# A fused attention and mixture-of-experts layer: keys and queries copied from SBUF into the stacks directly, and the experts' first gathers placed inside the last shared batch

## The chip, the cores and the metric

The kernel runs on 1 core of one Trainium2 chip. The metric is the device time of one execution in microseconds (us). PE is TensorE, DVE is VectorE, ACT is ScalarE, POOL is GpSimd and SP is SyncE, which here only issues DMAs.

## The reference

Input x has 8 sequences of 512 tokens with 512 features, all in float32.

```
h = layernorm(x)
c_kv, c_q = h @ W_DKV + b, h @ W_DQ + b                 # 128 wide each
k, q, v = c_kv @ W_UK + b, c_q @ W_UQ + b, c_kv @ W_UV + b   # 16 heads of 32
k_r, q_r = (h @ W_KR + b) * pe, (h @ W_QR + b) * pe     # 32 wide, shared by all heads
scores = concat(q, q_r) . concat(k, k_r) / sqrt(32)
x = x + layernorm(softmax(scores) @ v @ W_O + b)
h = layernorm(x)
shared = relu2(h @ shared_up) @ shared_down             # 512 -> 1024 -> 512
s = sigmoid(h @ router.T); pick 2 of 16 experts per token (2 of 4 groups first, by s + e_bias)
routed = sum over the 2 picked experts e of weight_e * relu2(h @ w_up[e]) @ w_down[e]   # 512 -> 256 -> 512
x = x + layernorm(routed + shared)
```

relu2 is the square of relu.

## The kernel before

**Stages.** Attention runs over 8 batches of 4 head groups (4 heads each), 32 groups u in all. Then the shared FFN runs over the first 4 batches ("shared batches"), the experts run over 79 tiles of 128 token rows sorted by expert, and the shared FFN of the last 4 batches runs together with the combination of the routed rows and the output. Products are made exact to nearly float32 by splitting operands into a high part (float32r) and a low part: three matmuls (`thrice`) for one.

**The order.** `K.order` is one list of steps, made by `attention_order`, `first_order`, `experts_order` and `combine_order`. Every engine's program walks the same list and issues its own instructions of each step, so the list sets the order on each engine and queue; semaphores do the rest. In attention `STEP` gives each side task the score step (0 to 31 within a group) beside which it stands; in the shared FFN `FIRST_STEP` gives it the number of the step (12 to a batch: 8 up-products, 4 down-products) after which it stands. Both tables are numbers written by hand or by a search.

**Keys and queries.** `half(u, "k")` and `half(u, "q")` make a group's K and Q on PE; ACT writes the high part and DVE the low part into `K.kq`, a single buffer [128, 4, 512]. Partition p = 32 j + d holds feature d of head j. The scores need stacks: `K.Kc` and `K.Qc`, three of each, with 128 partitions that are three 32-row pieces (high, high, low for K; high, low, high for Q) and 32 rows of the rotated part, for each of the 4 heads. `send(u)` on SP makes one: it copies `K.kq` to `kq_scratch` in DRAM (L1743), copies the rotated rows into the stacks (L1748, L1749) and, once the first copy has landed, reads the six pieces back in the new arrangement (L1753). Before the copies at L1748 it waits for the rotated part (`Z.rope`), which for the first group of a batch DVE makes (L888) while the third group of the batch before runs. ACT may write K of the next group into `K.kq` once the copy to DRAM has landed. `top(u)` (L614) multiplies queries and keys for the row maxima, which DVE reduces (L908); `scores(u)` (L628, L633) makes the scores, ACT the exponentials (L1404), POOL their sums (L1594).

**Choosing and inverting.** Beside the four shared batches DVE picks the experts ("choose early"), and computes every token's slot ("choose late"). Then eight steps "invert rows" (`spread`: L1218 to L1221 on DVE, eight small products of L757 on PE each) turn slots into the list of tokens for each expert tile, and "index" writes it (L1225). In the shared FFN L707 is the up-product (12 matmuls each), L729 the down-product (24 matmuls each); DVE makes the low part of each squared activation at L977.

**Experts.** `fetch(i)` on POOL gathers the 128 rows of a tile from DRAM (L1663), `move(i)` on SP copies them in four pieces within SBUF (L1828), DVE transposes (L1234), PE multiplies (L775, L798), the result goes to DRAM. Four buffers of each. The first fetches wait until the list is written and the up-products of the fourth shared batch are done, since their buffer lies in those activations' tile; the first transposition waits for the last down-product (`Z.dn`). Weights of the experts are loaded in groups: 0 and 1 (seven experts) beside the shared FFN, 2 and 3 (two experts each) at "weights 2" and "weights 3" on SP, the rest from ACT during the first ten tiles. The wait of a fetch and the head of `experts_order`:

```
        if i < 4:
            w.wait_ge(Z.idx, 1)
            w.wait_ge(Z.up, 8 * FIRST)
    out = [("fetch", i) for i in range(4)] + [("move", 0), ("move", 1)]
```

POOL also issues `store(b, i)`, which writes each shared result to DRAM (L1655) from one of two buffers; ACT waits for such a store before it reuses the buffer.

## Time and profile before

| | us |
|---|---|
| three runs, median (lowest to highest) | 1627.57 (1626.06 to 1628.75) |
| the profiled execution, its own time | 1631.91 |
| span of its profile | 1630.1 |
| PE busy in it | 1521.8 |
| DVE, ACT, POOL busy | 972.7, 786.2, 800.4 |
| mean granted clock of PE | 0.967 of full |

A busy share is a mean over stages with different limits. Attention lasts until about 909 us, the first four shared batches until 1115, the experts until about 1425, the rest is the second half of the shared FFN with the combination. In timelines the columns are start, duration, engine, line, operation, output and inputs, count; in brackets the idle time of the engine just before and what ended it. PEld is PE's weight load, SPq SP's DMA issues.

### The profile page before, as it was taken

How to read it: one execution, taken by the hardware profiler on the slowest of the kernel's cores; microseconds unless marked ns; L12 is line 12 of the kernel's file. 1: busy time of each engine (PE TensorE's matmuls, PEld its weight loads, DVE VectorE, ACT ScalarE, POOL GpSimd, SP SyncE). 2: the span in 40 equal slices, each digit the busy share in tenths (PEclk: the TensorE clock that was granted, in tenths of full speed). 3: DMA queues.
4: the chain of work that ended last, by engine and by line, in shares of the span. 5: the costliest groups of instructions: out<-in, count | busy, mean ns of one | idle time of the engine just before them, and what ended most of it. 6: DMA issues, size and time to landing. Idle time of an engine off the chain costs nothing.

```text
span 1630.1 us, 21821 instructions
## 1 busy us (share of the span) xinstructions
PE 1521.8 (93%) x7006; PEld 1034.3 (63%) x7006; DVE 972.7 (60%) x1871; ACT 786.2 (48%) x1417; POOL 800.4 (49%) x820
## 2 busy tenths in 40 slices
PE   4799999999999999999998999996899999969997
PEld 3465666656656566566564677875566666657886
DVE  3567676676756676757567336831333333339998
ACT  2355566456565665656647353430222222255554
POOL 1076696777776967768579430002222222133331
PEclk9799999999999999999999999998999999989999
DMA  4657358376483783745833334307977777596773
GB/s 118 192 146 203 101 163 253 104 223 175 129 223 107 196 253 113 214 142 150 279 106 105 129 129 144 109 20 246 289 215 214 213 224 211 160 338 221 225 233 130
DMA packets 169415, 291.32 MB, mean 179 GB/s; under 512 B 20596, under 2 KB 72692, under 8 KB 163156
## 3 DMA queue, kind: packets, MB, share of 16 engines
q1 hardware_dynamic: 150280, 242.21, 48.8%
q0 software_dynamic: 12912, 41.82, 8.7%
q10 hardware_dynamic: 6112, 5.90, 1.3%
q8 instruction: 58, 0.95, 0.2%
q14 instruction: 53, 0.43, 0.1%
HBM read 154.07 MB, written 92.01 MB: 151 GB/s over the span
## 4 chain that ended last, share of the span: by engine, by line
PE 75%; DMA 9%; DVE 4%; issue 4%; SPq 3%; POOL 3%; ACT 2%; DVEq 0%; POOLq 0%; ACTq 0%
PE bank L113 14%; PE bank L729 9%; PE bank L707 8%; PE bank L775 8%; PE bank L798 8%; PE bank L614 7%; PE bank L628 6%; PE bank L633 6%; PE bank L644 5%; DMA a<-kq_scratch 4%; PE bank L653 2%; SPq L1753 2%; POOL a L1594 2%; DMA kq_scratch<-a 1%; DMA f<-f 1%
## 5 line engine op out<-in xcount | busy, mean ns | idle before, releaser
L1594 POOL TENSOR_TENSOR a<-a 128x512 f32<-128x512 f32 x384 | 498.5, 1330 | 108.0 <-PE bank L653 68.6
L1404 ACT ACTIVATE a<-bank 128x512 f32<-128x512 f32 x512 | 298.4, 598 | 235.4 <-PE bank L633 183.8
L908 DVE TENSOR_REDUCE a<-bank 128x1 f32<-128x512 f32 x512 | 324.3, 680 | 79.5 <-PE bank L614 77.2
L113 PE MATMUL bank<-a 128*128 128x512 f32 (+1 forms) x864 | 245.0, 410 | 6.1 <-DVE a L854 4.0
L628 PE MATMUL bank<-a 128*128 128x512 f32 x512 | 222.0, 434 | 4.4 <-ACT a L1404 4.3
L614 PE MATMUL bank<-a 128*128 128x512 f32 x512 | 182.8, 429 | 29.6 <-DMA a<-kq_scratch 28.0
L633 PE MATMUL bank<-a 68*128 68x512 f32 x512 | 206.4, 403 | 0.7 <-ACT a L1394 0.6
L113 PEld LDWEIGHTS bank<-a 128*128 128x128 f32 (+1 forms) x864 | 166.0, 194 | 55.3 <-issue 10.3
L707 PE MATMUL bank<-c 128*128 128x512 f32 x768 | 181.4, 396 | 13.3 <-ACT c L1453 7.3
L729 PE MATMUL bank<-c 128*128 128x512 f32 x768 | 181.4, 396 | 4.5 <-DVE c L977 2.4
L1663 POOL DMA_INDIRECT f<-h_scratch,f x79 | 76.1, 963 | 208.5 <-DMA f<-f 206.6
L707 PEld LDWEIGHTS bank<-c 128*128 128x128 f32 x768 | 146.1, 191 | 48.0 <-issue 9.8
L729 PEld LDWEIGHTS bank<-c 128*128 128x128 f32 x768 | 145.7, 191 | 37.2 <-DVE c L977 3.3
L775 PE MATMUL bank<-f 128*128 x632 | 152.6, 385 | 17.9 <-DVE f L1234 16.6
L775 PEld LDWEIGHTS bank<-f 128*128 128x128 f32 x632 | 120.9, 193 | 70.2 <-issue 57.4
L628 PEld LDWEIGHTS bank<-a 128*128 128x128 f32 x512 | 98.4, 192 | 88.5 <-ACT a L1404 45.7
L614 PEld LDWEIGHTS bank<-a 128*128 128x128 f32 x512 | 98.4, 198 | 88.2 <-DMA a<-kq_scratch 32.2
L798 PE MATMUL bank<-f 128*128 x316 | 148.5, 593 | 0.0
L644 PE MATMUL bank<-a 128*32 128x512 f32 x1024 | 133.4, 607 | 0.0
L1242 DVE TENSOR_TENSOR f<-f 128x256 f32<-128x256 f32 x79 | 33.4, 423 | 138.1 <-ACT f L1518 138.0
L633 PEld LDWEIGHTS bank<-a 68*128 68x128 f32 x512 | 98.4, 192 | 18.8 <-ACT a L1394 4.8
L1528 ACT COPY f<-bank 128x512 f32<-128x512 f32 x79 | 46.3, 586 | 122.1 <-PE bank L798 122.1
(185 smaller groups left out, 1750.1 us busy)
## 6 DMA issues: line engine op xcount, KB each, us to landing
a<-kq_scratch SPq DMA_DIRECT2D x192, 256.0 KB, 5.7
kq_scratch<-a SPq DMA_DIRECT2D x32, 1024.0 KB, 4.1
a<-a SPq DMA_DIRECT2D x80, 256.0 KB, 5.4
f<-f SPq DMA_DIRECT2D x316, 64.0 KB
yp_scratch<-f SPq DMA_DIRECT2D x79, 256.0 KB, 3.2
a<-in_L_attn_x SPq DMA_DIRECT2D x15, 1024.0 KB, 8.4
x_scratch<-a SPq DMA_DIRECT2D x8, 1024.0 KB, 6.8
h_scratch<-a SPq DMA_DIRECT2D x8, 1024.0 KB, 12.4
```

Of the source, the lines that this page charges most:

```text
L113: t = e.matmul(out, a[n], b[n], start=n == 0 and m == 0, stop=n == len(ah) - 1 and m == 2)
L614: e.matmul(MX[n % 3][:], K.Qc[z][:, j, i * P:(i + 1) * P], K.Kc[z][:, j, :], start=True, stop=True).then_inc(Z.top, 1)
L628: e.matmul(SC[n % 2][:], K.Kc[z][:, j, i * P:(i + 1) * P], K.Qc[z][:, j, :], start=True, stop=False)
L633: e.matmul(SC[n % 2][:], K.KR[0:68, b % 2, j, i * P:(i + 1) * P], K.QR[0:68, u % 2, :], start=False, stop=True).then_inc(Z.score, 1)
L644: t = e.matmul(CT[HD * j:HD * j + HD, :], K.v[:, u % VS, i, HD * j:HD * j + HD], K.pt[:, n % NP, :], start=i == 0, stop=i == 3)
L707: t = e.matmul(bank[:], (K.sul if a else K.suh)[:, k, cut], (K.hTl if c else K.hTh)[:, k, :], start=m == 0, stop=m == 11)
L729: t = e.matmul(bank[:], (K.aTl if a else K.aTh)[:, k, cut], (K.sdl if c else K.sdh)[:, k, :], start=m == 0, stop=m == 23)
L775: t = e.matmul(K.UP[z][:, 0:FI], K.hTt[:, z, k * P:(k + 1) * P], K.flat[:, bass.ds(reg[i] + k * FI, FI)], start=k == 0, stop=k == 3)
L798: t = e.matmul(K.DN[z][:], K.eaT[:, z, k * P:(k + 1) * P], K.flat[:, bass.ds(reg[i] + 4 * FI + k * D, D)], start=k == 0, stop=k == 1)
L908: e.tensor_reduce(K.mx[:, i, j:j + 1], K.MX[n % 3][:], AX.X, ALU.max).then_inc(Z.max, 1)
L1404: e.activation(K.pt[:, n % NP, :], K.SC[n % 2][:], ACT.Exp, scale=SCALE).then_inc(Z.exp, 1)
L1594: e.tensor_tensor(K.acc[:, j, :], a, K.pt[:, n % NP, :], ALU.add).then_inc(Z.acc, 1)
```

## The change

The round trip through `kq_scratch` is gone. The columns of W_UK, W_UQ and their biases are permuted on the host so that partition p = 4 d + j holds feature d of head j; then a copy of 128 rows onto 32 partitions of four rows each is in the stack's order. `send(u)` first waits for the stack's last use, copies K's three pieces when K is drained, Q's three when Q is drained, and the two rotated copies last. ACT writes K of the next group only when all eight copies of the last stack have landed. The four first fetches, the weights of groups 2 and 3 and three moves are steps of `first_order` now (steps 40 to 45, in the fourth shared batch), with the weights issued by POOL instead of SP. All eight inversions stand at steps 33 to 35. Moves run three tiles ahead instead of two. Both tables of numbers are new.

```
@@ FIRST_STEP, STEP (numbers of most tasks differ by 0 to 5)
-        "weights": (44, 52, 56), "invert": (33, 33, 35, 35, 44, 44, 45, 45, 49)}
+        "weights": (37,), "invert": (33, 33, 34, 34, 34, 35, 35, 35, 37), "fetch": (40, 40, 40, 40, 41, 41, 41, 45, 45)}
@@ def first_order():
-                        ("early", [("choose early", 2)] * 26), ("late", [("choose late", 2)] * 34), ("weights", [("weights", n) for n in range(1, 4)]),
-                        ("invert", [("invert rows", n) for n in range(NCHUNK)] + [("index",)])):
+                        ("early", [("choose early", 2)] * 26), ("late", [("choose late", 2)] * 34), ("weights", [("weights", 1)]),
+                        ("invert", [("invert rows", n) for n in range(NCHUNK)] + [("index",)]),
+                        ("fetch", [("fetch", i) for i in range(4)] + [("weights", 2), ("weights", 3)] + [("move", i) for i in range(3)])):
@@ def experts_order():
-    out = [("fetch", i) for i in range(4)] + [("move", 0), ("move", 1)]
+    out = []
...
-            if i + 2 < NTILE:
-                out.append(("move", i + 2))
+            if i + 3 < NTILE:
+                out.append(("move", i + 3))
@@ scalar_program, half
-            w.wait_ge(Z.kq[(u - 1) % RS], 16 * ((u - 1) // RS + 1))
+            w.wait_ge(Z.stack[(u - 1) % RS], 8 * 16 * ((u - 1) // RS + 1))
@@ gpsimd_program
+    def weights(n):
+        if n < 2:
+            return
+        w.wait_ge(Z.inv, NCHUNK)
+        if n == 3:
+            w.wait_ge(Z.up, 8 * FIRST)
+        for e_ in range(E):
+            if GROUP[e_] == n:
+                for half in range(2):
+                    load_expert(e, K, ins, e_, half).then_inc(Z.ew[n], 16)
@@ sync_program, send
-        drained("half", u, "k")
-        drained("half", u, "q")
         if u >= RS:
             w.wait_ge(Z.stack[z], 8 * 16 * (u // RS))
-        e.dma_start(K.kq_d[z], raw(K.kq[:])).then_inc(Z.kq[z], 16)
+            w.wait_ge(Z.score, 16 * (u - RS + 1))
+        drained("half", u, "k")
+        for k, n in ((0, 0), (1, 0), (2, 1)):
+            e.dma_start(raw(K.Kc[z][HD * k:HD * k + HD, :, :]), raw(K.kq[:, n, :])).then_inc(Z.stack[z], 16)
+        drained("half", u, "q")
+        for k, n in ((0, 2), (1, 3), (2, 2)):
+            e.dma_start(raw(K.Qc[z][HD * k:HD * k + HD, :, :]), raw(K.kq[:, n, :])).then_inc(Z.stack[z], 16)
         rep = lambda r: raw(K.krx[r:r + HD, y, :].unsqueeze(1).broadcast_to([HD, 4, S]))
         w.wait_ge(Z.rope, 3 * (b + 1))
-        if u >= RS:
-            w.wait_ge(Z.score, 16 * (u - RS + 1))
         e.dma_start(raw(K.Kc[z][96:128, :, :]), rep(0)).then_inc(Z.stack[z], 16)
         e.dma_start(raw(K.Qc[z][96:128, :, :]), rep(32)).then_inc(Z.stack[z], 16)
-        piece = lambda n: K.kq_d[z, :, n, :].rearrange("(j p) s -> p j s", j=4)
-        w.wait_ge(Z.kq[z], 16 * (u // RS + 1))
-        for t, k, n in ((K.Kc, 0, 0), (K.Kc, 1, 0), (K.Kc, 2, 1), (K.Qc, 0, 2), (K.Qc, 1, 3), (K.Qc, 2, 2)):
-            e.dma_start(raw(t[z][HD * k:HD * k + HD, :, :]), piece(n)).then_inc(Z.stack[z], 16)
@@ sync_program, weights: groups 2 and 3 are gone
@@ kernel
+    for n in ("L0_attn_W_UK", "L0_attn_W_UQ", "L0_attn_b_UK", "L0_attn_b_UQ"):
+        given[n] = np.ascontiguousarray(given[n].reshape(-1, NG, 4, HD).swapaxes(2, 3).reshape(given[n].shape))
```

On SP, where the stack of a batch's first group is made (`a` are attention's tiles), before:

```order
L1743 DMA kq_scratch<-a 128x2048
L1748 DMA a<-a 32x4x512
L1749 DMA a<-a 32x4x512
L1753 DMA a<-kq_scratch 32x4x512 x6
L1727 DMA a<-a 32x4x512
L1728 DMA a<-a 32x4x512
L1717 DMA a<-in_L_attn_x 128x4x512
```

and now:

```order
L1753 DMA a<-a 32x4x512 x3
L1756 DMA a<-a 32x4x512 x3
L1759 DMA a<-a 32x4x512
L1760 DMA a<-a 32x4x512
L1736 DMA a<-a 32x4x512
L1737 DMA a<-a 32x4x512
L1726 DMA a<-in_L_attn_x 128x4x512
```

The six pieces stand ahead of the two rotated copies (L1759, L1760) and of the wait before them. On PE from the down-products of the third shared batch to the first expert tile, before:

```order
L729 MATMUL bank<-c 128x512 x48
L757 MATMUL bank<-h 128x79 x16
L729 MATMUL bank<-c 128x512 x48
L757 MATMUL bank<-h 128x79 x16
L707 MATMUL bank<-c 128x512 x96
L729 MATMUL bank<-c 128x512 x24
L757 MATMUL bank<-h 128x79 x16
L729 MATMUL bank<-c 128x512 x24
L757 MATMUL bank<-h 128x79 x16
L729 MATMUL bank<-c 128x512 x48
L773 TENSOR_LOAD f
```

and now:

```order
L730 MATMUL bank<-c 128x512 x48
L758 MATMUL bank<-h 128x79 x16
L730 MATMUL bank<-c 128x512 x24
L758 MATMUL bank<-h 128x79 x24
L730 MATMUL bank<-c 128x512 x24
L758 MATMUL bank<-h 128x79 x24
L708 MATMUL bank<-c 128x512 x96
L730 MATMUL bank<-c 128x512 x96
L774 TENSOR_LOAD f
```

All eight inversions (64 small products) stand in the third batch, none in the fourth. On POOL at the same place, before:

```order
L1655 DMA sh_scratch<-c 128x512 x12
L1663 DMA f<-h_scratch,f 128x512 x79
```

and now:

```order
L1653 DMA sh_scratch<-c 128x512 x8
L1661 DMA f<-h_scratch,f 128x512 x4
L547 DMA f<-in_L_ffn_w_up 128x4x256
L547 DMA f<-in_L_ffn_w_down 128x2x512
...
L1653 DMA sh_scratch<-c 128x512 x4
L1661 DMA f<-h_scratch,f 128x512 x75
```

Four gathers and eight weight loads (four pairs, of which one is shown) stand ahead of the fourth batch's four stores.

## Rows read from the trace of the kernel before

**Rows 1.** The page, busy time of each engine.
```profile
PE 1521.8 (93%) x7006; PEld 1034.3 (63%) x7006; DVE 972.7 (60%) x1871; ACT 786.2 (48%) x1417; POOL 800.4 (49%) x820
```
**Rows 2.** Who waited for whom on PE: us in all, times, longest.
```profile
PE bank L614 <- DMA a<-kq_scratch: 28.0, 10, 4.9
PE bank L729 <- DVE c L977: 2.4, 2, 1.4
```
**Rows 3.** Timeline, the prologue.
```profile
46.51 1.27 ACT L1387 ACTIVATE a<-bank,a 128x512 fp32r<-128x512 f32 x2 [1.00 <-DMA kq_scratch<-a]
...
53.83 2.29 DVE L854 TENSOR_TENSOR a<-s,a 128x2048 fp32r<-128x2048 f32 x1 [1.30 <-ACT a L1340]
...
56.75 9.54 PE L614 MATMUL bank<-a 128*128 128x512 f32 x16 [4.95 <-DMA a<-kq_scratch]
...
57.58 9.66 DVE L908 TENSOR_REDUCE a<-bank 128x1 f32<-128x512 f32 x16 [1.47 <-PE bank L614]
...
72.67 1.22 PE L614 MATMUL bank<-a 128*128 128x512 f32 x2 [2.81 <-DMA a<-kq_scratch]
```
**Rows 4.** Timeline, the end of attention, PE and POOL.
```profile
861.43 1.65 PE L614 MATMUL bank<-a 128*128 128x512 f32 x3 [2.99 <-DMA a<-kq_scratch]
...
870.07 1.28 POOL L1601 TENSOR_TENSOR s<-s,a 128x512 f32<-128x512 f32 x1 [1.18 <-DVE a L920]
```
**Rows 5.** Timeline of PE, from the shared FFN to the experts.
```profile
1103.47 11.15 PE L729 MATMUL bank<-c 128*128 128x512 f32 x48
...
1127.85 3.78 PE L775 MATMUL bank<-f 128*128 x8 [13.23 <-DVE f L1234]
...
1173.41 1.99 PE L775 MATMUL bank<-f 128*128 x8
```
**Rows 6.** Timeline of SP's queue, the stack of a batch's first group.
```profile
229.46 0.34 SPq L1743 DMA_DIRECT2D kq_scratch<-a  x1
236.55 0.60 SPq L1748 DMA_DIRECT2D a<-a  x1
...
237.84 3.86 SPq L1753 DMA_DIRECT2D a<-kq_scratch  x6
```
**Rows 7.** Timeline of PE, where that stack is asked for.
```profile
249.31 1.55 PE L614 MATMUL bank<-a 128*128 128x512 f32 x3 [2.53 <-DMA a<-kq_scratch]
```
**Rows 8.** DMA issues (KB each, median us to landing); landing times of all that touch kq_scratch.
```profile
a<-a SPq DMA_DIRECT2D x80, 256.0 KB, 5.4
...
DMA to landing us min/median/max: 3.5/5.5/13.0
```
**Rows 9.** The chain of waits around that stall: start, us, what.
```profile
231.73 2.78 PE bank L113 x12
...
250.85 2.37 PE bank L113 x6
```
**Rows 10.** Windows: PE, PEld, DVE, ACT, POOL busy, clock, DMA share, GB/s.
```profile
246.00:256.00 10.00, 7.47 (x34) 5.07 (x31) 4.58 (x8) 4.45 (x8) 3.26 (x3) 0.83 1.06 301
```
**Rows 11.** Timeline, inversions in the third and fourth shared batch.
```profile
1053.76 11.14 PE L729 MATMUL bank<-c 128*128 128x512 f32 x48
...
1055.43 1.22 DVE L1218 TENSOR_TENSOR h<-f 128x1024 f16<-128x1024 f32 x1
...
1070.20 0.69 DVE L977 TENSOR_TENSOR c<-c 128x512 fp32r<-128x512 f32 x1 [11.97 <-ACT c L1486]
...
1095.41 0.48 PE L757 MATMUL bank<-h 128*128 128x79 f16 x8 [2.23 <-DVE h L1221]
1095.72 7.30 PE L729 MATMUL bank<-c 128*128 128x512 f32 x24
```
**Rows 12.** The chain of waits, two expert tiles at full pace.
```profile
1184.66 1.73 PE bank L775 x8
...
1188.33 1.73 PE bank L775 x8
```
**Rows 13.** Timeline of POOL, the last store of the shared FFN.
```profile
1115.54 0.54 POOL L1655 DMA_DIRECT2D sh_scratch<-c  x1 [4.90 <-ACT c L1495]
```

More of the change, by code:

```diff
@@ L146 @@
 FIRST_STEP = {
-        "rest": (2, 2, 2, 3, 2, 2, 2, 3, 3, 5, 4, 5, 5, 7, 5, 6, 9, 9, 4, 9, 9, 9, 11, 9, 9, 9, 10, 10, 10, 10, 10, 10, 11, 13),
-        "prepare": (29,),
-        "early": (13, 13, 14, 14, 14, 14, 14, 15, 16, 17, 17, 18, 20, 20, 20, 20, 20, 20, 20, 21, 27, 28, 29, 31, 33, 35),
-        "late": (22, 22, 22, 22, 22, 22, 22, 22, 22, 22, 22, 23, 23, 23, 24, 24, 25, 25, 25, 25, 25, 25, 27, 27, 27, 27, 28, 28, 28, 29, 30, 30, 30, 36),
-        "weights": (44, 52, 56), "invert": (33, 33, 35, 35, 44, 44, 45, 45, 49)}
-STEP = {"split up": (4, 13, 17, 22, 25, 29, 36, 41), "split h": (38, 39, 42, 43), "last values0": 9, "total0": 8, "invert0": 5,
[11 rows of a table removed]
+        "rest": (1, 2, 2, 2, 2, 2, 3, 3, 3, 5, 5, 5, 7, 7, 5, 7, 9, 9, 5, 8, 8, 9, 11, 9, 9, 10, 10, 10, 10, 10, 10, 10, 11, 13),
+        "prepare": (33,),
+        "early": (13, 13, 14, 14, 15, 15, 16, 17, 17, 18, 18, 19, 19, 19, 20, 20, 21, 22, 22, 22, 23, 24, 24, 25, 25, 27),
+        "late": (22, 22, 22, 22, 23, 23, 23, 23, 23, 23, 23, 23, 23, 23, 23, 24, 24, 24, 24, 24, 24, 24, 24, 25, 25, 25, 25, 25, 25, 25, 26, 26, 28, 29),
+        "weights": (37,), "invert": (33, 33, 34, 34, 34, 35, 35, 35, 37), "fetch": (40, 40, 40, 40, 41, 41, 41, 45, 45)}
+STEP = {"split up": (5, 13, 17, 25, 28, 29, 35, 42), "split h": (38, 40, 41, 42), "last values0": 9, "total0": 8, "invert0": 7,
[11 rows of a table added]
 def beside_order(u):
@@ L357, in __init__ @@
             "x_in", "ident_in", "w1_in", "w1b_in", "w2_in", "w3_in"))
-        self.KR, self.kq, self.stack = many("KR_in", 2), many("kq_out", RS), many("stack_in", RS)
+        self.KR, self.stack = many("KR_in", 2), many("stack_in", RS)
         self.QR, self.w_hi, self.w_lo = many("QR_in", 2), make("w_high"), make("w_low")
@@ L947, in begun @@
             w.wait_ge(Z.stack[u % RS], 8 * 16 * (u // RS + 1))
-            w.wait_ge(Z.kq[u % RS], 16 * (u // RS + 1))
     def split_h(b, k):
@@ L1439, in begun @@
             w.wait_ge(Z.stack[u % RS], 8 * 16 * (u // RS + 1))
-            w.wait_ge(Z.kq[u % RS], 16 * (u // RS + 1))
     def passed():
@@ L1679, in gpsimd_program @@
     stages = {"scores": scores, "divide": divide, "root": root, "residual": residual, "split down": split_down, "choose early": choose,
-              "store": store, "fetch": fetch, "gather": gather}
+              "store": store, "fetch": fetch, "weights": weights, "gather": gather}
     for name, *at in K.order:
@@ L1808, in weights @@
     def weights(n):
+        if n > 1:
+            return
         if n == 0:
             over()
-        elif n == 1:
+        else:
             w.wait_ge(Z.slots, 2)
-        elif n == 2:
-            w.wait_ge(Z.inv, NCHUNK)
-        else:
-            w.wait_ge(Z.up, 8 * FIRST)
         for e_ in range(E):
@@ L1906, in program @@
     K.hT_d = dram("hT_scratch", [B, P, 4, S])
-    K.kq_d = dram("kq_scratch", [3, P, 4, S])
     K.shv = sh_d.rearrange("(t p) d -> t p d", p=P)
```

1 line of the change is left out of this document (removed), and 22 rows, old and new, of the table STEP.

## The prediction

> **What bounds it now.** I read the page first: TensorE (PE) is busy 1521.8 of 1630.1 us [rows 1], so time is to be had only where PE idles or runs at its lower clock. The list of who waited for whom gives the places. The largest is the first score product (L614) on the keys' and queries' stacks: 28.0 us in 10 waits [rows 2]. The timelines place them: one of 4.95 and one of 2.81 in the prologue [rows 3], one of 2.99 near the end of attention [rows 4]; the other seven hold 28.0 - 4.95 - 2.81 - 2.99 = 17.25 us, one in each batch but the last. Then comes the hand-over from the shared FFN to the experts: PE's last shared product ends at 1103.47 + 11.15 = 1114.6 and the first expert product starts at 1127.85, 13.23 us later [rows 5]. The rest (batches inside attention, experts' steady part, combine) the change leaves as it is.
>
> **Part 1: the seven stalls per batch.** In SyncE's (SP's) queue the stack of the next batch's first group goes so: copy to DRAM at 229.46, then a wait for the rotated keys until 236.55, two copies of those, and only at 237.84 the six reads from DRAM [rows 6]. PE asks for them at 249.31 - 2.53 = 246.78 [rows 7]. Now the six are issued before that wait, as soon as K and Q are drained, about 229.5 to 233, and only the two rotated copies follow at 236.55 to 237.8. With the median of such a copy, 5.4 us [rows 8], the last lands near 243, 4 us before PE asks. So the wait goes: 17.25 us. Behind it PE ran at its lower clock: six L113 matmuls took 2.37 us, where twelve take 2.78 at the full clock [rows 9], and the window around has a granted clock of 0.83, the lower of two levels (1.2 against 2.4 GHz) for part of it [rows 10]. Three L614 and six L113 took 1.55 + 2.37 = 3.92 us instead of 9 x 0.232 = 2.09: 1.83 lost, seven times 12.8. Together 30.1 us. The ends are 0, if the two rotated copies are themselves as late, and 31.
>
> What this costs elsewhere: the buffer K.kq is now free only when all eight copies of a stack have landed, where before one 1 MB write (some 4 us) freed it. In the loop the next group's K comes 18 us or more after the copies' issue (229.5 against 250), so ScalarE (ACT) doesn't wait. SP's new wait for the scores of three groups back stands ahead of the six copies; it is met at the group's first step, before K is made.
>
> **Part 2: the prologue.** Here the two halves follow each other closely. ACT made the second K at 46.51 [rows 3]; now it waits for the first stack, whose eight copies (issued 41 to 46.7) land at about 51.5. All behind it moves by those 5.0 us: the split of W_O on VectorE (DVE) ends at 61.1 instead of 53.83 + 2.29 = 56.1, and the 16 maxima, 9.66 us on DVE, end at 70.8 instead of 67.2 [rows 3]. In exchange the waits of 4.95 and 2.81 us are gone; the product that started at 72.67, 5.4 behind the maxima, starts 2.6 behind them at 73.4. Net 0.7 us lost (between 3.6 lost and 1 won).
>
> **Part 3: the end of attention.** The last stack's copies now start about 847 and end 851, so the last lands near 856, before PE asks at 861.43 - 2.99 = 858.4: the 2.99 us and about 2.6 of low clock (some 13 matmuls at 0.43 instead of 0.23) are gone from PE. But GpSimd (POOL) bounds there: its only idle piece before the following run of adds is 1.18 us [rows 4]. I take 1.2 us; 0 and 5.5 are the ends.
>
> **Part 4: choosing and inverting in the shared FFN.** The early steps of the choice are spread between the products' DVE steps instead of clumped: of two waits of 2.4 us in all [rows 2] I count 1.0 back (0 to 3.8 with the clock). The eight inversions are now all in the third shared batch. DVE ended the fourth one at 1070.20 - 11.97 = 1058.2 and then idled those 11.97 us; it took 2.8 (from 1055.43), so four more fit, the last ready at 1069.4 [rows 11]. But PE meets them earlier: two after the second down-product of this batch, three after the third (1053.76 + 5.5 = 1059.3, with the fifth ready at 1061.0) and three after the last. With some 0.3 us a group of eight small products that is 1.2 us of new wait and 2.0 behind it, and some 1.5 of low clock: 4.7. Before, the wait for DVE took 2.23 us and the products behind it 7.30 where 5.5 do [rows 11]: 4.0. I count 0 (3 lost to 4 won).
>
> **Part 5: the hand-over.** The last up-product of the fourth batch now ends near 1069.4 + 8 x 2.73 = 1091.3, and POOL issues the first four gathers then, beside the four down-products of 5.5 us each. Gathers, then the row copies (24 small copies, SP) have 22 us. What remains is the transposition, which waits for the last down-product because its tile lies in that data, and PE's load of the expert's address: 0.8 + 1.0 = 1.8 us; and the first expert product at the low clock, 3.78 instead of 1.99 us [rows 5]: 1.8. At full pace the twelfth tile starts 1.9 + 2.1 + 9 x 3.66 = 36.9 us after the first (two without a down-product, then 3.66 each) [rows 12]. To these I add 4 us: the fifth gather stands on POOL behind the last store of the shared output, so its tile is 1.5 late, and the late weights (512 KB a tile from ACT) still fill the DMA engines: 2.5. Sum 44.5, against 1173.41 - 1114.6 = 58.8 now [rows 5]: 14.3 won, between 8 (all stalls in the first tiles stay) and 19 (none). The eight weight loads moved to POOL stand behind the four gathers and ahead of four stores.
>
> A store of 128 rows costs POOL 0.54 us [rows 13]. If a load costs as much, the eight take 4.3 us; if the cost goes by rows, 3072 against 128, they take 13. Either way the first store leaves before 1110 and ACT, which needs its buffer back at 1108, is free by 1115, when the first expert result comes: no cost in the sum. The Trainium skill (DMA: Bandwidth & Descriptors, "Why a DMA increments its semaphore by 16 and not by 1") says that one descriptor moves one contiguous run, which speaks for the 13; by it too the sum is the same, but only some 4 us of room are left. No row here shows it.
>
> **Sum.** 30.1 - 0.7 + 1.2 + 1.0 + 0 + 14.3 = 45.9 us. The profiled execution took 1631.9 us and would take 1586.0; it lies 4.3 above the median of the three runs, 1627.6, from which the forecast is 1581.7: **1582 us**.
>
> **Rivals.**
> (a) The two rotated copies take the place of the wait. Landing times in this queue reach 13.0 us [rows 8]; issued at 237.8 in a stretch whose DMA share is 1.06 [rows 10], a copy that slow lands at 250.8 and the whole stall stays, 30.1 us dearer. For it: the x load, the KR copies and an h store are issued just behind. Against it: 1.5 MB are gone from in front of them. If half the stall stays: 1582 + 15 = 1597 us.
> (b) POOL's loads hold the hand-over up. From 17 us for the eight, ACT's last shared copies and the fifth gather come late by the excess; with 27 us part 5 wins 4 instead of 14: 1592 us. Only the 0.54 us row speaks of POOL's price.
> (c) Slower: the copies from SBUF to SBUF are slow. Before, 1 MB left SBUF in rows of 8 KB and came back from DRAM; now 1.5 MB are read from 128 partitions and written to 32 each. The place is every stack. The batch's fourth group has its copies issued at about 209.7 and PE asks at 223.9: 14 us; the first has 17, but its rotated copies only 10. If a set of eight takes 20 us, PE waits about 5.8 and 5.2 us a batch plus 3.6 of clock instead of 2.5 + 1.8: 10.3 more, seven times that is 72, less the 16 of the other parts: 1628 + 72 - 16 = 1684 us. It decides from about 16 us a set. Against it: the copies of the rotated rows are SBUF to SBUF already and take 5.4 us, as the reads from DRAM do, 5.5 [rows 8].
> The Trainium skill (SBUF — State Buffer, "Door 1: The DMA port swizzle") has a transfer's speed depend on how many of the 16 ports its partitions reach, and 32 partitions reach eight. If reads and writes shared them, 3.5 MB a set at its 435 GB/s would be 8 us by estimate, short of the 14; as the 5.4 us row agrees, it gives (c) little.
> (d) The new tables do nothing good and cost a wait of their own in each batch, so that nearly all of part 1 is spent again: no change.
>
> **Chances.** Forecast 0.66, (a) 0.16, (b) 0.12, (c) 0.04, (d) 0.02. The range, 1568 to 1601, reaches down to part 3 (4.3) and part 5 (4.7) at their upper ends with most of part 4's (6.8), and up past (b) and the halved stall of (a); beyond it lie the worse half of (a), (c) and (d). A measurement tells about 0.2% here, 3 us: faster 0.94, same 0.02, slower 0.04.
>
> **What would show it.** Part 1 right: no wait of L614 near the batches' ends, the granted clock 1.00 in the ten microseconds behind them, attention some 30 us shorter. (a): L614 waits for "a<-a". Part 2: the second K on ACT after 51. Part 4: two waits of L757 of 1 to 2 us before the fourth shared batch, none within it. Part 5: under 4 us of idle between the last shared and the first expert product; (b) would show as ACT waiting for a store. Wrong altogether: a new wait of PE in every group, or a set of eight copies beyond 14 us.

## The result: 1611.4 us, 1% faster, 29 us above the forecast

The changed kernel takes 1611.4 us (median of 4 runs, 1610.7 to 1612.4), the kernel before 1628.1 in the same session. The ratio is 0.9903, 95% interval 0.9888 to 0.9918: 15.8 us off 1627.6, 13 to 18. Forecast were 46 us and a range from 1568 to 1601. The profiled execution took 1610.7 us with a span of 1608.9, against 1631.9 and 1630.1 before: 21.2 us between the two profiles, some 5 more than between the medians. Below, "gain" is always (1 - ratio) x 1627.6, and places in the trace are compared between profiled executions.

The page of the changed kernel, busy time and the first DMA queue, and the issues of the stacks' copies (KB each, median us to landing):
```profile
PE 1508.8 (94%) x7006; PEld 1026.4 (64%) x7006; DVE 966.2 (60%) x1871; ACT 782.8 (49%) x1417; POOL 807.6 (50%) x828
...
q1 hardware_dynamic: 142472, 204.46, 56.5%
...
a<-a SPq DMA_DIRECT2D x272, 256.0 KB, 8.4
```
And the same queue before:
```profile
q1 hardware_dynamic: 150280, 242.21, 48.8%
```
The queue moves 38 MB less than before and its packets take more of the DMA engines' time. The copies land 8.4 us after their issue, where those of [rows 8] took 5.4. These two rows hold most of the surprise, all that comes ahead of the hand-over.

Who waited for whom on PE, after (us in all, times, longest), beside [rows 2]:
```profile
PE bank L607 <- DVE a L896: 13.0, 1, 13.0
PE bank L615 <- DMA a<-a: 9.2, 8, 2.3
...
PE bank L776 <- issue: 6.8, 1, 6.8
```
The 28.0 us on the stacks are down to 9.2, but a wait of 13.0 has come in the prologue and one of 6.8 among the experts. The timeline places them: first the prologue (ACT, PE, DVE), beside [rows 3],
```profile
57.57 1.26 ACT L1387 ACTIVATE a<-bank,a 128x512 fp32r<-128x512 f32 x2 [12.43 <-DMA a<-a]
```
```profile
59.16 6.18 PE L607 MATMUL bank<-s,a 128*128 128x512 f32 x8 [13.00 <-DVE a L896]
```
```profile
69.58 9.65 DVE L909 TENSOR_REDUCE a<-bank 128x1 f32<-128x512 f32 x16
```
ACT writes the second K at 57.57 instead of 46.51, because it waits for the first stack's eighth copy, and the sixteen maxima end at 79.2 instead of 67.2: 12.0 us are lost before the loop begins. Why, the chain of waits tells, here for a stack inside the loop (issue of the first copy of Q at 219.04, the set begun at 217.04):
```profile
219.04 0.58 SPq L1756
...
220.96 0.65 SPq L1759
...
221.65 12.19 DMA a<-a
233.84 0.04 issue
233.89 0.98 PE bank L615 x3
```
and the windows, in the prologue while one set moves, and in the loop:
```profile
44.00:56.00 12.00, 2.17 (x9) 1.06 (x7) 0.00 (x0) 0.75 (x2) 0.00 (x0) 0.77 1.07 137
222.00:230.00 8.00, 8.00 (x43) 5.01 (x42) 4.47 (x7) 3.53 (x7) 8.00 (x7) 1.00 1.08 128
```
A set needs 16.8 us from its first issue to its last landing (16.9 in the prologue), and in both windows the DMA engines are full (share 1.07 and 1.08) at 137 and 128 GB/s. The 301 GB/s of [rows 10] are no measure of the stacks' reads from DRAM: the x load (issued at 243.10) and an h store (243.82) are in flight there. Over 238 to 246, with the six reads under way, the kernel before moved 208 GB/s at a share of 0.97. PE asks for this stack at 232.9. So the wait of a batch has not gone; it has moved from the first group's stack to the fourth group's and is 0.65 to 1.50 us instead of 1.9 to 3.5 (seven waits, 6.9 us in all); the eighth, at the last stack, is 2.35 us where it was 2.99. PE's clock no longer falls behind the seven: over 100 to 800 us the granted clock is 1.00 (before 0.98) and PE is busy 691.9 us of 700 (before 681.5):
```profile
100.00:800.00 700.00, 691.89 (x3611) 442.28 (x3610) 484.02 (x838) 429.56 (x769) 532.21 (x527) 1.00 0.77 140
```
the same of the kernel before:
```profile
100.00:800.00 700.00, 681.53 (x3481) 437.18 (x3480) 476.77 (x819) 417.74 (x742) 517.87 (x513) 0.98 0.61 175
```
From the prologue's 12.0 behind, the kernel comes to be 8.4 us ahead at the last stack (853.04 against 861.43), 11.6 ahead at the last shared product (1103.0 against 1114.6 [rows 5]) and 21.2 ahead at the combination. In the last step the hand-over gives 9.6 us. PE's timeline there:
```profile
1104.86 5.40 PE L776 MATMUL bank<-f 128*128 x16 [1.82 <-DVE f L1234]
...
1116.30 1.88 PE L799 MATMUL bank<-f 128*128 x4
1124.99 3.78 PE L776 MATMUL bank<-f 128*128 x8 [6.81 <-issue]
```
The wait ahead of the first tile is 1.82 us, as forecast; the fifth tile then waits 6.81 us, and its first products run at the lower clock, 3.78 us instead of 1.89. POOL and ACT show what its rows waited for:
```profile
1087.19 0.84 POOL L547 DMA_DIRECT2D f<-in_L_ffn_w_up  x1
...
1092.46 0.76 POOL L547 DMA_DIRECT2D f<-in_L_ffn_w_down  x1
1093.15 1.19 POOL L1653 DMA_DIRECT2D sh_scratch<-c  x2
1106.94 0.55 POOL L1653 DMA_DIRECT2D sh_scratch<-c  x1 [12.60 <-ACT c L1494]
1107.77 0.54 POOL L1653 DMA_DIRECT2D sh_scratch<-c  x1 [0.28 <-issue]
1108.61 1.00 POOL L1661 DMA_INDIRECT f<-h_scratch,f  x1 [0.30 <-issue]
```
```profile
1105.95 0.58 ACT L1494 COPY c<-bank 128x512 f32<-128x512 f32 x1 [13.16 <-DMA sh_scratch<-c]
```
The eight loads cost POOL 6.0 us, but the first store, issued behind their 4 MB, lands only at 1105.9; ACT waits for it with its next copy, POOL waits for ACT with the third store, and the fifth gather stands behind that.

### The profile page after: what moved, and what is told of

Same layout as the page of the kernel before. It is cut to its first block, busy times and chain, and to the rows that moved or that the text cites. A ratio compares the mean times of both kernels' runs of the same rounds, so it can differ in the third digit from the quotient of the medians.

```text
span 1608.9 us, 21774 instructions
## 1 busy us (share of the span) xinstructions
PE 1508.8 (94%) x7006; PEld 1026.4 (64%) x7006; DVE 966.2 (60%) x1871; ACT 782.8 (49%) x1417; POOL 807.6 (50%) x828
## 3 DMA queue, kind: packets, MB, share of 16 engines
q1 hardware_dynamic: 142472, 204.46, 56.5%
## 4 chain that ended last, share of the span: by engine, by line
PE 75%; DMA 8%; DVE 6%; ACT 4%; issue 4%; POOL 2%; SPq 2%; DVEq 0%; POOLq 0%; ACTq 0%
PE bank L113 11%; PE bank L708 9%; PE bank L776 9%; PE bank L799 8%; PE bank L730 7%; DMA a<-a 7%; PE bank L629 7%; PE bank L615 6%; PE bank L645 6%; PE bank L634 6%; PE bank L654 2%; PE bank L788 1%; ACT a L1347 1%; SPq L1756 1%; POOL a L1593 1%
## 5 line engine op out<-in xcount | busy, mean ns | idle before, releaser
L1404 ACT ACTIVATE a<-bank 128x512 f32<-128x512 f32 x512 | 295.1, 598 | 241.5 <-PE bank L634 190.5
L113 PE MATMUL bank<-a 128*128 128x512 f32 (+1 forms) x864 | 236.3, 398 | 6.2 <-DVE a L855 4.0
L629 PE MATMUL bank<-a 128*128 128x512 f32 x512 | 221.8, 433 | 6.2 <-ACT a L1404 5.8
L113 PEld LDWEIGHTS bank<-a 128*128 128x128 f32 (+1 forms) x864 | 159.5, 187 | 53.3 <-issue 10.3
L708 PE MATMUL bank<-c 128*128 128x512 f32 x768 | 181.2, 396 | 13.1 <-ACT c L1452 6.9
L615 PE MATMUL bank<-a 128*128 128x512 f32 x512 | 176.2, 422 | 15.8 <-DMA a<-a 9.2
L730 PE MATMUL bank<-c 128*128 128x512 f32 x768 | 178.0, 391 | 4.5 <-DVE c L967 2.1
```

The lines of the kernel that those rows point to most:

```text
L113: t = e.matmul(out, a[n], b[n], start=n == 0 and m == 0, stop=n == len(ah) - 1 and m == 2)
L615: e.matmul(MX[n % 3][:], K.Qc[z][:, j, i * P:(i + 1) * P], K.Kc[z][:, j, :], start=True, stop=True).then_inc(Z.top, 1)
L629: e.matmul(SC[n % 2][:], K.Kc[z][:, j, i * P:(i + 1) * P], K.Qc[z][:, j, :], start=True, stop=False)
L708: t = e.matmul(bank[:], (K.sul if a else K.suh)[:, k, cut], (K.hTl if c else K.hTh)[:, k, :], start=m == 0, stop=m == 11)
L730: t = e.matmul(bank[:], (K.aTl if a else K.aTh)[:, k, cut], (K.sdl if c else K.sdh)[:, k, :], start=m == 0, stop=m == 23)
L1404: e.activation(K.pt[:, n % NP, :], K.SC[n % 2][:], ACT.Exp, scale=SCALE).then_inc(Z.exp, 1)
```

## The experiments

Two theories stood at the start. **T1**: the copies' pace (a set keeps the DMA engines for 16 to 17 us) costs the prologue and keeps the wait. **T2**: the copies are well enough, and the one buffer held for all eight of them, the order or the tables cost it. For the hand-over: **G**, the fifth gather's place; **D**, the traffic of the weights.

| run | edit, to the changed kernel unless told | us | ratio, 95% interval | gain |
|---|---|---|---|---|
| the change | | 1611.4 | 0.9903 (0.9888 to 0.9918) | 15.8 |
| a1 | to the kernel before: direct copies alone | 1617.5 | 0.9933 (0.9917 to 0.9948) | 10.9 |
| a2 | stacks through DRAM as before | 1618.7 | 0.9938 (0.9919 to 0.9957) | 10.1 |
| a3 | a2, six reads ahead of the rotated copies | 1631.4 | 1.0022 (1.0009 to 1.0035) | -3.6 |
| a4 | a2, so in each batch's first group alone | 1593.4 | 0.9790 (0.9771 to 0.9809) | 34.2 |
| t2 | K's half of the buffer freed early | 1606.2 | 0.9877 (0.9861 to 0.9894) | 20.0 |
| h1 | gathers 5 to 7 ahead of the third store | 1605.9 | 0.9872 (0.9856 to 0.9888) | 20.8 |
| h2 | POOL's loads behind two stores | 1613.1 | 0.9920 (0.9904 to 0.9936) | 13.0 |
| h3 | ACT's late weights two tiles later | 1610.3 | 0.9890 (0.9873 to 0.9907) | 17.9 |
| b1 | a4, gathers 5 to 7, then the loads, after two stores | 1588.9 | 0.9753 (0.9734 to 0.9772) | 40.2 |
| b2 | b1 with h3 | 1586.7 | 0.9741 (0.9719 to 0.9762) | 42.2 |
| d1 | stacks' rows interleaved | 1592.9 | 0.9765 (0.9751 to 0.9778) | 38.2 |
| d2 | d1 with the hand-over of b2 | 1586.5 | 0.9728 (0.9714 to 0.9742) | 44.3 |
| d3 | b2 with interleaved rows | 1584.2 | 0.9727 (0.9705 to 0.9748) | 44.4 |

**The two parts of the change.** In a1 only `send`, ACT's wait and the permuted columns are taken over:
```
-            w.wait_ge(Z.kq[(u - 1) % RS], 16 * ((u - 1) // RS + 1))
+            w.wait_ge(Z.stack[(u - 1) % RS], 8 * 16 * ((u - 1) // RS + 1))
```


> One part alone: the kernel before with nothing but the direct copies (old tables, weights and gathers where they were). Theory 1 (a set of eight direct copies keeps the DMA engines for 16 to 17 us, twice what the reads from DRAM take, so the prologue loses 12 us and the stall per batch only shrinks): the second K on ACT after 57 us instead of 46.5, seven stalls of L614 about 1 us or moved to another stack, attention some 8 us shorter in all, so 1628 - 8 = 1620 us (1614 to 1626). Rival, my forecast's own (the copies are as quick as the reads, the loss in the prologue came from the new tables): second K at 51 us, no wait in the batches, 1628 - 30 = 1598 us.

> The other part alone: the changed kernel with the keys and queries going through DRAM again in the old order (new tables, gathers and weights in the last shared batch stay). The trace of the changed kernel is 21.2 us ahead at its end: 8.4 at the end of attention, 3.2 more in the shared FFN, 9.6 in the hand-over. Theory 1: the first 8.4 belong to the copies, so this one takes 1628 - 13 = 1615 us (1611 to 1619), with the wait of L614 in each batch back at 2 to 3 us and the prologue's K at 46.5. Rival (the tables themselves cure the stalls): 1603 us or below.

a1 gains 10.9 us and a2 10.1. a1 shows the changed kernel's prologue and loop with the old tables: the second K at 57.96, one wait of 0.70 to 1.51 us a batch at the fourth group's stack, 4.38 at the last stack, the last stack's products 7.2 us earlier.
```profile
57.96 1.27 ACT L1386 ACTIVATE a<-bank,a 128x512 fp32r<-128x512 f32 x2 [12.31 <-DMA a<-a]
```
a2 has the old waits (1.7 to 3.1 us a batch, 24.5 in all with the prologue's) and the new hand-over with its wait of the fifth tile, 7.8 us. So the tables are cleared of the prologue's loss. The parts add up to 21 us and the change shows 15.8. These 5 us are hardly clear of the noise: the intervals are 2.4 to 3.1 us on each number, some 4.7 on the difference. The spans of the profiled executions add up to 24.4 (11.8 and 12.6) against 21.2. What of it is real, and why, stays open.

**The price of a copy by itself.** m1, m2 and m3 compute nothing (the output is a copy of an input); SP issues sets of six copies of 256 KB, each set when the one before has landed.

> The disputed cost by itself: no computation at all (the output is a copy of the input). SyncE alone issues sets of six copies of 256 KB, each set after the one before has landed: the direct form (128 partitions to 32), one such copy alone, the same rows as 24 copies of 32 partitions to 32 in the old order of channels, the reads from DRAM, 32 partitions read four times over, 128 partitions to 128, write to DRAM then reads, and half a set each way. Theory 1: 1.5 MB in the direct form take 12 us or more (about 125 GB/s), the reads from DRAM 5 to 6 us (about 290), the repeated rows about 7.5 (205). If what slows is only SBUF as the source, 128 to 128 is as slow as the direct form (12 us); if it is the spread of the source rows over partitions against 32 destinations, 128 to 128 is quick and the ordered form quick too. Rival (the copies are slow in the kernel only through other traffic): all forms within 20% of each other, 5 to 7 us a set.

SP's issues, the first copy of each set:
```profile
10.11 2.01 SPq L36 DMA_DIRECT2D direct<-source  x3
...
24.45 0.55 SPq L36 DMA_DIRECT2D single<-source  x1
...
44.97 1.28 SPq L36 DMA_DIRECT2D fromdram<-round_scratch  x3
...
54.76 2.15 SPq L36 DMA_DIRECT2D repeated<-source  x3
...
64.25 1.84 SPq L36 DMA_DIRECT2D plain<-source  x3
...
70.02 0.35 SPq L36 DMA_DIRECT2D round_scratch<-source  x1
```
and the windows in the middle of the direct, DRAM, repeated and plain sets (POOL busy, clock, DMA share, GB/s):
```profile
12.00:22.00 10.00, 0.00 (x0) 1.00 1.07 126
47.00:53.00 6.00, 0.00 (x0) 1.00 0.95 216
57.00:63.00 6.00, 0.00 (x0) 1.00 1.01 224
66.00:69.00 3.00, 0.00 (x0) 1.00 1.01 382
```
T1 stands: 1.5 MB in the direct form take 14.3 us (10.11 to 24.45) with nothing beside them. The reads from DRAM take 9.8 (I had expected 5 to 6), the repeated rows (the form of the rotated copies) 9.5, and 128 partitions to the same 128 only 5.8. So SBUF as a source is not slow; this form is. Write and reads together took 13.6 us (write 3.9, from 70.02 to 73.91, reads 9.7): **the direct way is no shorter than the way through DRAM**. The 24 small copies told nothing of the pace; SP's issues (0.63 us each) set it.

> The cost by itself again, no computation (the output is a copy of the input); sets of six copies of 256 KB inside SBUF. The first such run gave 126 GB/s for the direct form (128 partitions to 32, rows of 2 KB), 224 for 32 partitions read four times into 32, 382 for 128 to 128. Here: the direct form again, 32 to 32 partitions with 8 KB each, 128 to 64 partitions, 32 (8 KB each) to 128, and the direct form with three copies on SyncE's queue and three on ScalarE's. If the number of destination partitions sets the pace, 32 to 32 is at most 224 and 128 to 64 between 126 and 382 (about 200 to 250), and 32 to 128 near 382. If it is the change of partition between source and destination, 128 to 64 and 32 to 128 are slow too (about 130). If it is the one queue, the last set takes 8 us instead of 14.

128 to 64 partitions went at 129 GB/s, as slow as the direct form (128); 8 KB rows from 32 to the same 32 at 236, 32 to 128 at 217; two queues instead of one gave 139. It is neither the one queue nor 32 as such.

**Order.** The six reads ahead of the wait for the rotated keys (a3), and so in each batch's first group alone (a4, here):
```
+        late = u % NG == 0 and u > 0
+        if not late:
+            rotated()
...
         for t, k, n in ((K.Kc, 0, 0), (K.Kc, 1, 0), (K.Kc, 2, 1), (K.Qc, 0, 2), (K.Qc, 1, 3), (K.Qc, 2, 2)):
             e.dma_start(raw(t[z][HD * k:HD * k + HD, :, :]), piece(n)).then_inc(Z.stack[z], 16)
+        if late:
+            rotated()
```
(`rotated` is the wait for `Z.rope` and its two copies; a3 has it behind the six reads in every group.)


> As the run before, but the six reads from DRAM are issued as soon as the write has landed, ahead of the wait for the rotated keys, the two rotated copies behind. Theory 1 (order was worth what the forecast said, the new source of the copies spoilt it): no wait in the batches, no low clock behind them, prologue as before, so about 28 us less than the run before: 1587 us (1583 to 1594). Rival (the two rotated copies, or the round trip of 4 + 6 us, keep the wait): within 8 us of the run before, 1607 to 1615, with L614 waiting for a rotated copy. Rival 2 (what the loop won in the changed kernel came from the direct path being short, not from order): waits of 1 to 3 us stay in each batch.

> The changed kernel with keys and queries through DRAM again, but the order of SyncE's copies by group: in each batch's first group the six reads go ahead of the wait for the rotated keys; in the other three the two rotated copies go first, while the write to DRAM is under way. Seen so far: with rotated copies first always, only the first group's stack is late (2 to 3 us a batch); with them last always, only the fourth's (2 to 3 us). Theory (each wait is one of order: a direct set, 14.3 us alone, is no quicker than the write and the reads, 13.6, but needs no wait for SyncE in between): neither wait is left, the prologue stays as before, so 1618.7 - 7 x 3 = 1598 us (1594 to 1604). Rival (the stack is simply ready too late whatever the order, because a set takes 10 us or more of the queue): one wait a batch of 1.5 us or more remains, 1609 to 1620 us.

a3 fell out against me: 1631.4 us. The first group's wait is gone, but in the fourth group, and in the prologue, PE now waits for a rotated copy. SP's queue of a3 shows it:
```profile
215.05 0.34 SPq L1755 DMA_DIRECT2D kq_scratch<-a  x1
219.02 2.68 SPq L1761 DMA_DIRECT2D a<-kq_scratch  x6
221.74 0.64 SPq L1764 DMA_DIRECT2D a<-a  x1
```
SP stands still from 215.4 to 219.0 until its write has landed. The old order had the two rotated copies in that gap, for nothing; it was wrong only where the rotated keys are late, in one group of four. a4 does each where it belongs and gains 34.2 us with the copies through DRAM, so what the direct copies won in the loop can be had by order alone. Only two waits of over 0.6 us for a stack are left behind the prologue (1.09 at 630.18, and 2.76 at the last stack, which starts at 834.15, 27.3 us ahead of before).

**The buffer held.**
```
-            w.wait_ge(Z.stack[(u - 1) % RS], 8 * 16 * ((u - 1) // RS + 1))
+            w.wait_ge((Z.kin, Z.stack)[n][(u - 1) % RS], (3, 5)[n] * 16 * ((u - 1) // RS + 1))
```


> The changed kernel with a semaphore of their own for the three copies of K: ScalarE writes the next K once those three have landed, and the next Q once the other five have, where it waited for all eight. Theory T1 (the copies' pace is what costs: 126 GB/s, 6 us for the K copies, 14 to 16 for the set): second K at about 49 instead of 57.6, but the second set can't move before the first is through, so the prologue gets back only part, 3 to 6 of 12 us: 1606 to 1609 us. Theory T2 (the loss of 12 us is only the buffer held for the last copy): nearly all of it returns, 1600 us. If the order of the split of W_O behind the second Q decides, nothing returns: 1611.

```profile
49.21 0.69 ACT L1391 ACTIVATE a<-bank,a 128x512 fp32r<-128x512 f32 x1 [3.91 <-DMA a<-a]
57.61 0.69 ACT L1391 ACTIVATE a<-bank,a 128x512 fp32r<-128x512 f32 x1 [7.71 <-DMA a<-a]
```
K comes at 49.2, as T1 said, but Q only at 57.6. The maxima end at 72.0, 7 us earlier, and some 4 us arrive in the time (gain 20.0 against 15.8; the two intervals just overlap). Holding the buffer costs what the copies' pace makes it cost.

**The place of the rows.**

> The cost by itself, no computation (the output is a copy of the input); sets of six copies of 256 KB: the direct form onto 32 partitions in a row, the same onto every fourth partition, reads from DRAM onto 32 in a row and onto every fourth, 8 KB rows from every fourth partition to the same one, and 8 KB rows from 32 partitions to the next 32. Theory P (the place of the destination rows sets the pace: 32 in a row share half the ways into SBUF): every fourth partition takes the direct form from 126 GB/s to 220 or more, and the reads from DRAM from 216 towards 380; the shifted copies stay near 220. Theory F (the form, 128 source rows onto 32 partitions, is what is slow wherever they lie): the direct form stays at 126 on every fourth partition.

SP's issues again, and windows in the middle of the direct form, the same onto every fourth partition, DRAM onto 32 in a row, DRAM onto every fourth:
```profile
24.19 1.84 SPq L36 DMA_DIRECT2D spread<-source  x3
...
29.97 1.90 SPq L36 DMA_DIRECT2D dramnarrow<-round_scratch  x3
```
```profile
12.00:22.00 10.00, 0.00 (x0) 1.00 1.08 129
26.00:29.00 3.00, 0.00 (x0) 1.00 1.02 380
32.00:38.00 6.00, 0.00 (x0) 1.00 0.96 211
43.00:47.00 4.00, 0.00 (x0) 1.00 0.90 289
```
The same 1.5 MB from the same rows take 5.8 us instead of 14.3 when they are written to every fourth partition. Rows of 8 KB from every fourth partition to the same ones went at 352 GB/s, from 32 partitions to the next 32 at 248. Set into the changed kernel (d1), with the stacks' 128 rows in another order, over which the products sum anyway:
```
-            e.dma_start(raw(K.Kc[z][HD * k:HD * k + HD, :, :]), raw(K.kq[:, n, :])).then_inc(Z.stack[z], 16)
+            e.dma_start(raw(K.Kc[z][k:P:4, :, :]), raw(K.kq[:, n, :])).then_inc(Z.stack[z], 16)
...
```
(Q's copies take the same rows, the two rotated ones every fourth from 3.)

> The changed kernel with one thing else: the stacks' rows are interleaved, piece k of a stack on partitions k, k + 4, k + 8 ... instead of 32 in a row; the products sum over all 128 partitions, so their order is free. Theory P: a set takes 8 to 10 us instead of 16.9 in the prologue, so ScalarE's second K comes at 50 to 51 us instead of 57.6, the wait in each batch goes, 1611.4 - 7 - 8 = 1596 us (1592 to 1600). Theory F: nothing changes, 1611 us.

d1, the queue and the issues, ACT in the prologue, and the loop:
```profile
q1 hardware_dynamic: 142472, 204.46, 40.5%
...
a<-a SPq DMA_DIRECT2D x272, 256.0 KB, 3.0
```
```profile
50.24 1.26 ACT L1387 ACTIVATE a<-bank,a 128x512 fp32r<-128x512 f32 x2 [4.78 <-DMA a<-a]
```
```profile
100.00:800.00 700.00, 698.85 (x3648) 447.26 (x3647) 490.07 (x849) 430.71 (x770) 534.99 (x529) 1.00 0.46 142
```
Same packets, same bytes, 40.5% of the engines' time instead of 56.5; the copies land after 3.0 us; PE waits for no stack in the loop and is busy 698.9 us of 700. Another order of rows, in four lines, is worth 22 us (gain 38.2 against 15.8). As the sets are quick, ACT's wait shrinks to 4.8 us though the buffer is held as before.

**The hand-over.**
```
h1:  ("fetch", 4..6) at step 46, ahead of the third store
h2:  ("weights", 2), ("weights", 3) at step 46 instead of 41
h3:  if 2 <= i < len(LATE) + 2: out.append(("late weights", i - 2))
```


> The changed kernel with the fifth to seventh gathers on GpSimd moved ahead of the third store of the last shared batch (before: behind the fourth, issued at 1108.6). Theory G (the 6.8 us that TensorE waits at the fifth tile come from that gather's place behind stores which wait for ScalarE's buffer): fifth gather issued about 1095, its wait gone, 1611.4 - 7 to 9 = 1603 us (1601 to 1606), ScalarE's wait of 13.2 us for the first store's landing unchanged. Rival D (the DMA engines are full, share 1.05, with 4 MB of weights and then the late weights, so the tiles' data come late whatever is issued when): the wait moves by under 2 us, 1609 to 1612 us.

> The changed kernel with the eight weight loads on GpSimd moved behind the first two stores (before: ahead of them). If the stores' landing (12.8 us) is queueing behind those 4 MB, ScalarE's wait of 13.2 us for the first store goes, the third store leaves at 1099 to 1100 instead of 1106.9, the fifth gather at about 1105.5 instead of 1108.6. Theory G: the fifth tile's wait shrinks by those 3 us, 6.8 to about 4, and 1611.4 becomes about 1608 us. Rival D (traffic): weights now land up to 1112 and collide with the fifth gather, so the wait stays at 7 or grows, 1611 to 1614 us.

> The changed kernel with the ten late weight loads on ScalarE begun two tiles later. In the trace of the changed kernel the DMA engines are busy at a share of 1.05 to 1.09 from 1112 to 1124, while the fifth gather (issued at 1108.6) and the row copies behind it are under way; the earlier gather brought 5.5 us back and left a wait of 3.6. Theory D (traffic of the late weights is the other part of the wait): the fifth tile's wait shrinks from 6.8 to about 3, the time from 1611.4 to 1607 to 1608 us, no new wait at tiles 11 to 14. Rival G (the gather's place alone): the wait stays at 6 to 7 us, 1611 us.

h1 takes the fifth tile's wait from 6.8 to 3.6 us and gains 5 us more than the change. So the place counts, as G said, though the wait isn't gone, as G also said it would be. What is left of it is in its chain:
```profile
1096.35 12.44 DMA f<-h_scratch,f
...
1111.07 9.19 DMA f<-f
```
the gather, issued behind the 4 MB on the same queue, lands 12.4 us later, and the last row copy 9.2 us after its issue. These row copies (L1833) go from 128 partitions to 32 in a row as well, the form that is slow in m1, with rows of 512 bytes instead of 2 KB; spreading them wasn't tried. h2 shows the queueing itself: with the stores ahead of the loads ACT's wait of 13.16 us is gone and the third store leaves at 1099.2. But its own fifth gather (1104.6) is behind the loads all the same, the tile still waits 5.3 us, and the time is not better (1613.1 us, where G wanted 1608; the interval overlaps the change's). h3 shortens the wait to 4.1 us in its profile; in the time it can't be told from the change. So only the gather's place shows in the times. That stores and gathers queue behind the loads is seen in the traces, but h2 bought no time with it, and the late weights' traffic shows in the waits alone.

> Towards a version that beats both: the order by group through DRAM (1593.4 us; its fifth tile waits 7.6 us), and in the hand-over gathers five to seven and then the weight loads both between GpSimd's second and third store. If place and queueing are what the two runs showed (earlier gather 5.5 us, weights behind the first stores 0 to 1.5), the wait of the fifth tile falls to 2 to 4 us and the time to 1588 us (1586 to 1590). Rival D: with the weights now landing up to 1097 or so, the gathered rows still come late, 1591 to 1593.

> As the run before, with the late weight loads begun two tiles later too. Theory D: another 2 to 3 us, no wait over 1 us left at the fifth tile, 1585 us. Rival G: no difference from the run before, 1588 us. If the late weights then miss their own tiles, a new wait of TensorE at the twelfth to fourteenth tile, 1590 or more.

> The run before with the earlier gathers, the weights behind the second store and the late weights two tiles later. These brought 6.7 us on the way through DRAM (1593.4 to 1586.7). Theory P: 1596 - 7 = 1589 us. Theory F: 1604 us. It is the version in which all that the change meant to do would be done by direct copies; if it stays above the 1586.7 of the way through DRAM, the buffer held through the prologue is what remains.

> The best so far (through DRAM, order by group, hand-over mended; 1586.7 us) with interleaved stacks. Theory P: the six reads take some 5 us instead of 8 to 10, the first two stacks' waits in the prologue (together some 6 us with the one at 73) shrink, 1582 to 1585 us. Theory F: 1586.7, within 2 us.

b1 gains 6 us over a4; its fifth tile waits 3.2 us, and two later ones 0.9 and 1.5. In b2's profile the fifth doesn't wait and no other waits over 1.2, which points at the late weights' traffic as the rest of that wait (D), by one profile each; b1 and b2 can't be told apart by their times. d2 and d3 have the lowest medians, 44 us below the kernel before and 28 below the change; they can't be told apart either, nor from b2 (42.2), so that interleaved rows help the way through DRAM isn't shown. The direct copies, placed well, and the way through DRAM, ordered well, come to the same: neither has a wait for a stack in the loop, though d3 keeps one of 2.3 us at the last stack, and in the prologue the held buffer costs d2 5.3 us at L607 where d3 waits 1.2 there and 6.0 for its first stack.

## Why the prediction was wrong

**The step that failed** is in Part 1 and again in Part 2: "With the median of such a copy, 5.4 us [rows 8], the last lands near 243". The eight copies of a set, six of them direct, were taken to land some 5 us after the last issue; they landed 12.2 us after it, 16.8 us after the first issue. The row quoted was that of another form: the rotated copies go from 32 partitions to 32 (224 GB/s in m1), the new ones from 128 to 32 in a row (126 GB/s). And the median was read of one copy, where the stack needs the last of eight that share the DMA engines: in the changed kernel a copy of K, at the head of the set, lands after 5.7 us (median, L1753), the second rotated copy, at its end, after 12.1 (L1760). The kernel before has one kind of transfer in the new form, the experts' row copies (L1828, 128 partitions to 32 in a row, rows of 512 bytes); I didn't look at them for it.

Of the forecast's 45.9 us the profiled executions show 21.2. Ahead of the hand-over 20.0 are missing (31.6 forecast, 11.6 measured); quick copies bring back 16.4 of them (d1 is 28.0 ahead at the last shared product), which is this step. In the hand-over 4.7 are missing, the step named at Part 5. The other 5.4 lie between the profiled pair and the medians (21.2 against 15.8).

**Rival (c) was the case**, with its place, and I gave it 4%. It said "decides from about 16 us a set" and reckoned with 20; the set took 16.9, just past the edge, so the loop was still won in part and the 1684 us of (c) stayed away. What I took for strong evidence against it was the same 5.4 us row. The Trainium skill (SBUF — State Buffer, "Door 1: The DMA port swizzle") says that speed depends on how many of the 16 ports the partitions reach, that partitions 0 to 63 reach no more of them than 0 to 31, and I made 8 us a set of it by estimate. The first half agrees with m1 to m3: 211 to 248 GB/s into 32 partitions in a row where the source lies in as many or in DRAM, 128 to 64 no quicker than 128 to 32, and 380 onto every fourth partition. The estimate does not. It took the page's full 435 GB/s, though 32 partitions reach half of the ports; half of 435 would be 218, or 9.6 us for the 2 MB written, by estimate, and even so the direct form has 126 to 129 (while two of the others, 236 and 248, lie above 218). On every fourth partition a row's source also lies within four partitions of its destination; whether that nearness or the number of ports gives the 380 these runs can't say, and why the direct form falls below even the reads from DRAM (216) stays open.

**Part 1**, 30.1 us: the loop won back 20.4 (12.0 behind to 8.4 ahead). With quick copies (d1) it is 28.5: from 3.8 behind, maxima ending at 71.1, to 24.7 ahead at the last stack (836.73). The mechanism was right, also that the low clock behind the seven waits goes with them; the size hung on the copy. One more term was too high: the 1.83 us of low clock was read at one stall and taken seven times, but at two of the seven (569.45 and 675.36) the same three products took 0.97 and 1.04 us, not 1.55. How much of the 12.8 us that costs wasn't measured.

**Part 2**, 0.7 us lost: 12.0 lost. In d1, where a set lands about when I had assumed, the second K comes at 50.2 (forecast after 51), the split of W_O ends at 61.5 (61.1) and the maxima at 71.1 (70.8). The exchange, the waits of 4.95 and 2.81 us, was had, but 11 us late instead of 5.

**Parts 3 and 4**, 1.2 + 1.0 us: 3.2 between the last stack and the last shared product. Part 3's mechanism failed by the same step: the last stack's copies, issued from 836.17 on, have landed only at 853.0, so 2.35 of the 2.99 us of wait stayed, and the clock behind it still falls (granted 0.85 over 853 to 863, before 0.69 over 861 to 871). In d1 PE doesn't wait for this stack. The two waits of the inversions are there as forecast, 0.92 and 1.49 us. The two parts weren't separated.

**Part 5**, 14.3 us by the start of the twelfth tile: 9.1 there (at 1152.77, 49.7 behind the last shared product instead of 44.5), 9.6 at the combination. The first tile's wait is 1.82 (forecast 1.8). The failed term is "To these I add 4 us": the fifth tile cost 6.81 of wait and 1.89 of low clock, 8.7 in its place, which is 4.7 of the 5.2 missing. I had put the fifth gather behind the last store and made it 1.5 late; I hadn't asked when ACT gets its buffer back from a store that is queued behind 4 MB of weights. **Rival (b)** looked at the wrong resource: the loads cost POOL 6.0 us, far from the 17 that would decide, but their bytes stand in its queue. Of the price per load: 512 rows cost 0.84 us and 256 rows 0.76, against 0.54 for 128 [rows 13], so it doesn't go by rows, and the 13 us that I drew from the Trainium skill (DMA: Bandwidth & Descriptors, "Why a DMA increments its semaphore by 16 and not by 1") were too many.

**Rival (a)** stayed away in the change, but a3 is its picture: rotated copies behind the six, with a wait of 1.9 to 3.1 us a batch for them, because through DRAM the write's landing stands in between. The sign that I gave for (a), a wait for "a<-a", can't tell it from (c), since all eight copies are "a<-a" now; the place does, the fourth group's stack and not the first's. **Rival (d)** was not the case: the tables alone (a2) add no wait in the batches, and 9.6 of the 12.6 us of their profile come behind the last shared product.

With both repairs the change is where the forecast had it: d2's ratio on 1627.6 is 1583.3 us, against 1582. That the numbers meet so closely is in part luck, since d2 also moves three gathers and the late weights, which the forecast didn't count.

## What to carry to other kernels

Price a transfer by a row of the same form: the same partitions on both sides, the same row length, and as many in flight; where there is none, measure a set of them by itself. A removed trip through DRAM saves nothing by itself if what replaces it moves the same bytes more slowly, and a copy that gathers 128 partitions into a narrow block is better spread over every fourth partition if the consumer sums over them anyway. Before work is put on another engine's queue, ask what stands behind it in that queue, transfers that wait for a buffer above all, and not only what its issue costs.

## What was not expected of the hardware

- The same six copies take 14.3 us onto partitions 0 to 31, 32 to 63, 64 to 95, and 5.8 us onto every fourth partition (129 against 380 GB/s, DMA share 1.08 and 1.02). Reads from DRAM gain less: 211 to 289 GB/s.
- 128 to 64 partitions in a row (129 GB/s) is as slow as 128 to 32.
- A 256 KB store issued on POOL behind eight loads of 512 KB lands about 12.8 us later; with the stores ahead of the loads ACT no longer waits for them.
